# Convolution block with two position networks: first step ahead of its chunk, a place for each chunk of x, and a new order of the loads in the last stretch

## The reference

```
def srms(x): return x / (norm(x) * d ** (-0.5) + EPS)

xn = srms(x)
u = silu(xn @ u_w.T + u_b)              # 96 -> 288 channels
v = silu(xn @ v_w.T + v_b)
a1, a2 = rpe_net(positions, ...)        # two small networks, 256 wide, 3 layers, 128 positions each
out = conv_along_height(v, a2) + conv_along_width(v, a1)   # per channel, by FFT in the reference
out = u * out
return out @ o_w.T + o_b + x
```

## Time and profile before

| | before |
|---|---|
| time, median of 3 runs | 815.77 us (814.77 to 816.03) |
| the profiled execution's own time | 814.11 us |
| its span | 812.3 us |
| PE busy | 749.5 us (92%) |
| ACT busy | 533.9 us (66%) |
| DVE busy | 470.2 us (58%) |
| POOL busy | 282.6 us (35%) |
| moved by DMA | 161.11 MB, mean 198 GB/s |

### The profile page before, as it was taken

One profiled execution on the slowest core, in us unless ns is written; L12 is line 12 of the kernel. 1 busy time (PEld: TensorE's weight loads), 2 busy tenths in 40 slices (PEclk: granted clock), 3 DMA queues, 4 the chain that ended last, 5 costly groups with the idle time before them and its releaser, 6 DMA issues.

```text
span 812.3 us, 19208 instructions
## 1 busy us (share of the span) xinstructions
PE 749.5 (92%) x7148; PEld 672.2 (83%) x7148; DVE 470.2 (58%) x845; ACT 533.9 (66%) x866; POOL 282.6 (35%) x187
## 2 busy tenths in 40 slices
PE   0999997998999999899999999989999998987887
PEld 0999886988999998799999999979999998765655
DVE  6566542336898886444444454445455553776666
ACT  0566574775666666677777877746666666655554
POOL 4333333212212112655555555410000001966764
PEclk9999998999999999999999999989999999999999
DMA  9555554369889786488988888776555555688786
GB/s 209 159 156 156 156 134 138 160 199 215 187 193 200 160 187 191 144 272 272 270 271 262 266 275 271 231 202 144 133 134 131 136 134 185 200 250 248 247 262 193
DMA packets 132017, 161.11 MB, mean 198 GB/s; under 512 B 69484, under 2 KB 97132, under 8 KB 131948
## 3 DMA queue, kind: packets, MB, share of 16 engines
q1 hardware_dynamic: 131948, 160.15, 70.6%
HBM read 109.49 MB, written 50.63 MB: 197 GB/s over the span
## 4 chain that ended last, share of the span: by engine, by line
PE 75%; DMA 13%; DVE 4%; issue 2%; POOL 2%; SPq 2%; ACT 1%; ACTq 0%; DVEq 0%; POOLq 0%
PE ps L974 22%; PE ps L1049 15%; PE ps L1021 9%; PE ps L1034 9%; DMA out<-x_e 9%; PE ps L994 7%; PE ps L984 6%; PE ps L965 3%; DMA stage<-a_dram 2%; PE ps L997 1%; POOL u_in L504 1%; DMA u_dram<-u_in 1%; SPq L300 1%; PE ps L948 1%; DMA free_rows<-in_x 1%
## 5 line engine op out<-in xcount | busy, mean ns | idle before, releaser
L504 POOL TENSOR_TENSOR u_in<-u_in,v 128x1152 f32<-128x1152 f32 (+2 forms) x66 | 174.6, 2651 | 177.5 <-DMA u_in<-u_dram 161.0
L876 DVE TENSOR_TENSOR g<-ps,g 128x512 fp32r<-128x512 f32 (+1 forms) x192 | 125.7, 681 | 74.9 <-ACT g L571 45.8
L832 DVE COPY toepB<-stage 64x512 f32<-64x512 f32 x144 | 105.2, 730 | 80.1 <-PE ps L1049 72.6
L1049 PE MATMUL ps<-toepB,vt 128*128 128x128 f32 x1152 | 141.8, 277 | 0.9 <-POOL toepB L488 0.5
L1049 PEld LDWEIGHTS ps<-toepB,vt 128*128 128x128 f32 x1152 | 136.3, 194 | 1.4 <-POOL toepB L488 0.7
L974 PE MATMUL ps<-wu,xh 97*128 97x288 f32 x512 | 123.6, 307 | 2.1
L766 DVE TENSOR_TENSOR xl<-ps,xh 96x512 fp32r<-96x512 f32 x64 | 43.9, 687 | 140.5 <-ACT xh L544 140.5
L974 PE MATMUL ps<-wv,xh 97*128 97x288 f32 x512 | 120.8, 311 | 2.3 <-ACT u_in L548 1.3
L984 PE MATMUL ps<-ident,u_in 128*128 128x128 f32 (+1 forms) x768 | 102.2, 276 | 21.3 <-POOL u_in L504 20.3
L984 PEld LDWEIGHTS ps<-ident,u_in 128*128 128x128 f32 (+1 forms) x768 | 81.7, 127 | 36.8 <-DVE g L876 12.7
L548 ACT ACTIVATE v<-ps 128x576 f32 (+1 forms) x128 | 83.5, 652 | 38.2 <-PE ps L974 28.7
(11 more groups left out here) (79 smaller groups left out, 1006.5 us busy)
## 6 DMA issues: line engine op xcount, KB each, us to landing
stage<-a_dram SPq DMA_DIRECT2D x144, 256.0 KB, 4.3
u_in<-u_dram SPq DMA_DIRECT2D x64, 576.0 KB, 5.3
u_dram<-u_out SPq DMA_DIRECT2D x48, 576.0 KB, 3.3
x_e<-in_x_eT SPq DMA_DIRECT2D x64, 192.0 KB, 3.8
out<-x_e SPq DMA_DIRECT2D x64, 192.0 KB, 3.8
u_dram<-u_in SPq DMA_DIRECT2D x16, 576.0 KB, 2.8
x_n<-in_x SPq DMA_DIRECT2D x16, 384.0 KB, 5.4
xa<-in_x SPq DMA_DIRECT2D x64, 96.0 KB, 4.6
```

What stands on the lines that cost most here:

```text
L504: return nc.gpsimd.tensor_tensor(out=tile, in0=tile, in1=v[:, start // 2:end // 2, bass.ds(t * NB, NB)].rearrange("p c n e -> p n c e"), o ...
L832: nc.vector.tensor_copy(toepB[n % 2][rows, :, rows], stage[n % STAGES][rows, axis].rearrange("p k c -> p c k")[:, :, ::-1]).then_inc(toepB ...
L876: nc.vector.tensor_tensor(out=low, in0=ps[0:w, bank], in1=high.bitcast(f32), op=ALU.subtract).then_inc(gl_ready, 1)
L1049: last = nc.tensor.matmul(ps[:, SET_BANK[n % 2] + c // NB, (c % NB) * P:(c % NB + 1) * P], vt[n % 2][:, c], toepB[n % 2][:, c], start=Fals ...
```

## The change

Three edits, and a renumbering of counters that follows from them.

1. Start. Chunk 0 is loaded in two parts: step 0 alone (`x_first_loaded`), then steps 1 to 3. DVE squares, sums and norms step 0 by itself (batch 0), and PE projects it as soon as v's weights are split; steps 1 to 3 are a second batch. The position rows (`r_h`) and `rpe_square`, which stood ahead of and right behind the first norms on DVE, come after the second batch. POOL scales step 0 first and then squares steps 1 and 2 of chunk 0; DVE squares step 3. PE's `project(0)` is ahead of `transpose_x(1)` and `rpe_part(0, 0)`, and ACT's `high_x(1)` behind the silus of step 0. All counts of `norms_summed` and `norms_ready` rise by one.
2. A place of its own for each late chunk: chunk 4 in rows of v's space behind the weights (columns that are written from step 20 on), chunks 5, 6, 7 in three places in `x_late`. Chunk 7 is loaded in `phase_a(4)`, without the wait for the scalings.
3. Last stretch. SP's body is now: load u of step t + 3, store the result of step t - 2, wait for the store of step t - 4, load x_e of step t.

```diff
@@ -88,7 +88,8 @@
         OB = OW + 2 * RC * NCH
         RH = OB + 2 * NCH
         RSQ, RIN, W_RAW = RH + 2 * RC, RH + 4 * RC, RH + 6 * RC
-        assert W_RAW + 2 * NCH <= D // 2
+        X_FREE = W_RAW + 2 * NCH
+        assert X_FREE + CHUNK_ROWS <= D // 2
 
         def lw_row(n, o, layer, c):
             return LW + ((n * RC + o) * LAYERS + layer) * RC + c
@@ -112,13 +113,16 @@
 
         g = place("g", [P, 5, TOK], V + 36864, f32r)
         g1 = [place(f"g1{k}", [P, 5, TOK], V + 26624 + 12288 * k, f32r) for k in range(2)]
-        x_late = [place(f"x_late{k}", [P, CHUNK_ROWS, E], V + offset) for k, offset in enumerate((36864, 13824, 0))]
+        x_late = [place(f"x_late{k}", [P, CHUNK_ROWS, E], V + offset) for k, offset in enumerate((0, 13824, 36864))]
 
         def x_chunk(c):
 
             if c < FREE_CHUNKS:
                 return rows(CHUNK_ROWS * c, CHUNK_ROWS, E)
-            return x_late[(c - FREE_CHUNKS) % 3][:]
+            if c == FREE_CHUNKS:
+
+                return free_rows[:, X_FREE:X_FREE + CHUNK_ROWS, 1, P - E:P]
+            return x_late[c - FREE_CHUNKS - 1][:]
 
         x_n = place("x_n", [P, CH * NB, E], V + 22528)
 
...
@@ -246,7 +250,11 @@
                 for i in range(2):
                     sp.dma_start(x_chunk(c)[H * i:H * i + H], rows_of(0, CH * c, CH, i)).then_inc(x_all_loaded, 16)
 
-            load_x_all(0)
+
+            for first, steps, loaded in ((0, 1, x_first_loaded), (1, CH - 1, x_all_loaded)):
+                for i in range(2):
+                    sp.dma_start(x_chunk(0)[H * i:H * i + H, NB * first:NB * (first + steps)],
+                                 rows_of(0, first, steps, i)).then_inc(loaded, 16)
             sp.dma_start(r_pw[:, 0], pos_w).then_inc(pos_loaded, 16)
             sp.dma_start(r_pw[:, 1], pos_b).then_inc(pos_loaded, 16)
             for n, (weight, bias) in enumerate(((v_wT, v_b), (u_wT, u_b))):
...
@@ -319,12 +327,8 @@
                                  ).then_inc(stage_loaded[k], 16)
 
             def phase_a(c, first, last):
-                if c + 3 < CHUNKS - 1:
+                if c + 3 < CHUNKS:
                     load_x_all(c + 3)
-                elif c + 2 == CHUNKS - 1:
-
-                    sp.wait_ge(x_scaled, CH * (c + 2 - 2))
-                    load_x_all(c + 2)
                 for r in range(CH):
                     if last and r == 2:
                         sp.wait_ge(a_stored, 32)
...
@@ -401,12 +405,11 @@
                         if not (first and r == 0) and not (last and r > 0):
                             sp.wait_ge(y_transposed, NCH * STEPS + NCH * t)
                             load_u(1, t + 3, r + 3)
-                        if not (first and r < CH - 1) and not (last and r == CH - 1):
-                            up = (r + 1) // CH
-                            sp.wait_ge(o_stored[1][(r + 1) % CH], 16 * c + 16 * up)
-                            load_xe(1, t + 1, r + 1)
                         if not first or r >= 2:
                             store_out(1, t - 2, r + 2)
+                        if not first:
+                            sp.wait_ge(o_stored[1][r], 16 * c)
+                            load_xe(1, t, r)
                 for c in range(CHUNKS):
                     body(c, c == 0, c == CHUNKS - 1)
                 for t in range(STEPS - 2, STEPS):
@@ -443,12 +446,12 @@
                 nc.gpsimd.tensor_tensor(out=xa[r % 2][:], in0=source, in1=factor, op=ALU.mult).then_inc(x_scaled, 1)
 
             def scale_a0(t, c, r):
-                pool.wait_ge(norms_ready, c + 1)
+                pool.wait_ge(norms_ready, c + 2 if t else 1)
                 wait(pool, x_transposed, t - 1)
                 scale(t, x_chunk(c)[:, NB * r:NB * (r + 1)], r)
 
             def scale_a1(t, loads, chunk, r):
-                pool.wait_ge(norms_ready, CHUNKS + chunk + 1)
+                pool.wait_ge(norms_ready, CHUNKS + chunk + 2)
                 pool.wait_ge(xa_loaded[r % 2], 32 * loads)
                 scale(STEPS + t, xa[r % 2][:], r)
 
@@ -456,25 +459,27 @@
                 nc.gpsimd.tensor_tensor(out=target, in0=source, in1=source, op=ALU.mult).then_inc(squared, 1)
 
             def square_a0(c, r):
-
-                if r == 0:
+                if r == 0 or c == 0:
                     pool.wait_ge(x_all_loaded, 32 * (c + 1))
-                    wait(pool, norms_summed, c)
+                    pool.wait_ge(norms_summed, c + 1)
                 square(x_chunk(c)[:, NB * r:NB * (r + 1)], x_sq[:, NB * r:NB * (r + 1)])
 
             def square_a1(j):
                 pool.wait_ge(xn_loaded, 32 * (j + 1))
                 square(x_n[:], x_n[:])
 
-            for r in range(2):
+
+            scale_a0(0, 0, 0)
+            for r in range(1, CH - 1):
                 square_a0(0, r)
             for r in range(CH - 2):
                 square_a0(1, r)
 
             def phase_a(c, first, last):
                 for r in range(CH):
-                    scale_a0(CH * c + r, c, r)
-                    if first and r == 0:
+                    if not (first and r == 0):
+                        scale_a0(CH * c + r, c, r)
+                    if first and r == 1:
                         square_a0(1, CH - 2)
                         square_a0(1, CH - 1)
                     if c < CHUNKS - 2:
@@ -575,12 +580,15 @@
             def phase_a(c, first, last):
                 for r in range(CH):
                     t = CH * c + r
-                    if not (last and r == CH - 1):
+                    start = first and r == 0
+                    if not start and not (last and r == CH - 1):
                         high_x(t + 1, r + 1)
                     for pair in range(2):
                         silu_v(0, t, pair)
                     for pair in range(2):
                         silu_u(0, t, pair, u_tile(0, r), ua_stored[r % 2], 16 * (2 * c + r // 2) if isinstance(c, int) else 32 * c + 16 * (r // 2))
+                    if start:
+                        high_x(1, 1)
             chunks(act, phase_a)
 
             def phase_c(half):
...
@@ -718,16 +713,16 @@
                 nc.vector.reduce_sum(n_tmp[:, 0, 0:steps * NB], x2, axis=AX.X).then_inc(norms_summed, 1)
 
             def sum_a0(c):
-                sum_squares(CH, x_sq[:], c, CH * (c + 1))
+                sum_squares(CH, x_sq[:], c + 1, CH * (c + 1) - 1)
 
             def sum_a1(j):
-                sum_squares(CH, x_n[:], CHUNKS + j, CH * CHUNKS + j + 1)
+                sum_squares(CH, x_n[:], 1 + CHUNKS + j, CH * CHUNKS + j)
 
             def norms_a0(c, layer=None):
-                return norms(CH * c, CH, c, layer)
+                return norms(CH * c, CH, c + 1, layer)
 
             def norms_a1(j):
-                return norms(STEPS + CH * j, CH, CHUNKS + j)
+                return norms(STEPS + CH * j, CH, 1 + CHUNKS + j)
 
             def run(pieces):
                 for piece in pieces:
@@ -766,9 +761,15 @@
                 nc.vector.tensor_tensor(out=xl[r % 2][0:E], in0=ps[0:E, bank], in1=xh[r % 2][0:E].bitcast(f32),
                                         op=ALU.subtract).then_inc(xl_ready, 1)
 
-            sum_a0(0)
-            run(norms_a0(0))
-            rpe_square()
+            def square_x(r):
+                x_step = x_chunk(0)[:, NB * r:NB * (r + 1)]
+                return nc.vector.tensor_tensor(out=x_sq[:, NB * r:NB * (r + 1)], in0=x_step, in1=x_step, op=ALU.mult)
+
+
+            dve.wait_ge(x_first_loaded, 32)
+            link(square_x(0))
+            nc.vector.reduce_sum(n_tmp[:, 0, 0:NB], x_sq[:, 0:NB], axis=AX.X).then_inc(norms_summed, 1)
+            run(norms(0, 1, 0))
 
             dve.wait_ge(weights_loaded, 4 * 16)
             for n, w in enumerate((wv, wu)):
@@ -777,7 +778,24 @@
                 nc.vector.tensor_copy(high, raw).then_inc(w_split, 1)
                 dve.wait_ge(w_split, 2 * n + 1)
                 nc.vector.tensor_tensor(out=low, in0=raw, in1=high.bitcast(f32), op=ALU.subtract).then_inc(w_split, 1)
-            low_x(0, 0)
+                if n == 0:
+                    dve.wait_ge(x_all_loaded, 32)
+                    square_x(CH - 1).then_inc(squared, 1)
+                    low_x(0, 0)
+
+
+            dve.wait_ge(squared, CH - 1)
+            nc.vector.reduce_sum(n_tmp[:, 0, 0:(CH - 1) * NB], x_sq[:, NB:CH * NB], axis=AX.X).then_inc(norms_summed, 1)
+            run(norms(1, CH - 1, 1))
+
+            dve.wait_ge(pos_loaded, 2 * 16)
+            dve.wait_ge(positions, 2)
+            for n in range(2):
+                for c in range(RC):
+                    last = nc.vector.tensor_scalar(r_h[:, n, c], r_pos[:], r_pw[:, 0, n, c:c + 1],
+                                                   r_pw[:, 1, n, c:c + 1], ALU.mult, ALU.add)
+            link(last)
+            rpe_square()
 
             def phase_a(c, first, last):
                 networks = isinstance(c, int) and c <= LAYERS
@@ -1000,17 +1018,24 @@
             pe.wait_ge(consts_ready, 3)
```

(30 more changed lines are left out.)

## The result

| | before | changed |
|---|---|---|
| median of the runs | 815.27 us | 788.43 us (787.38 to 791.33) |
| ratio | | 0.9681 (0.9648 to 0.9715) |
| the profiled execution, its span | 814.11, 812.3 us | 791.33, 789.5 us |

The change makes the kernel 3.2% faster, 26.0 us by the ratio. The forecast was 797.2 us in a range of 788 to 806, so the time lies at the lower end of the range, outside the likeliest case's own 794 to 801, and nearest to the rival in which PE sets the last stretch (792.3). The profiled execution of the changed kernel is the slowest of its four, that of before one of the faster ones: between the two spans lie only 22.8 us.

The account below looks back on a forecast made before the run. The prediction took the last stretch to be held by a 4.05 us circle of output store and x_e load on SP. Terms: -16.6 + 0.3 - 3.3 + 1.0 = -18.6 us, from 815.77 to 797.2 us, range 788 to 806.

Parts of the forecast that it names:

- the likeliest case: Last stretch: DMA sets a step at 3.02 to 3.3 us; 794 to 801 us in total, chance 0.48.
- the rival in which PE sets the last stretch: Last stretch: PE limits a step at 2.945 us, 21.5 us less there; 792.3 us in total, chance 0.28.
- The circle in the last stretch: SP's load of x_e waits for an output store issued one body before, 4.05 us a step; the new order removes it.
- Its size: Last stretch: 24 steps fall from 3.84 to 3.15 us each, 16.6 us less.
- One sign that I had named for being wrong: DMA: the prediction is wrong if the queue carries more than 334 GB/s.
- my second case: Last stretch: at 425 GB/s DMA would need 2.3 us a step, and PE would set it at 2.945.
- Landings: Last stretch, rival: x_e and u land late, 5.75 us, a step takes 3.5 us; 805.6 us in total, chance 0.19.
- Chunk 7: Its earlier load removes 7.9 us of pause and cold clock, adds 2.6 and 2.0: 3.3 us less.
- The start: Step 0 is projected earlier, but step 1 waits for chunk 2: no gain, 1.0 us more (0 to +2.5).
- The 0.3 for the very end: End of the last stretch: the last x_e is issued some 3 us ahead of use, landing 3.5: 0.3 us more.

Follow-up runs that it names:

- last_only: The kernel before with the third edit alone (SP's order in the last stretch): 792.63 us, ratio 0.9712 to the kernel before.
- short_pe: The changed kernel with one of three matmuls left out for both full blocks of the last stretch's output projection: 785.93 us, ratio 0.9649 to the kernel before.
- x_e_twice: The changed kernel with every load of x_e in the last stretch from step 4 on made twice: 806.56 us, ratio 0.9908 to the kernel before.
- place_only: The kernel before with the second edit alone (a place for each late chunk, chunk 7 loaded one chunk sooner): 812.40 us, ratio 0.996.
- early_seven: The changed kernel with chunk 7 loaded ahead of the store of the networks' result instead of behind it: 792.24 us, ratio 0.9713 to the kernel before.
- late_square: The changed kernel with POOL scaling step 2 before its first square of chunk 2: 790.16 us, ratio 0.9695 to the kernel before.
- split_store: The changed kernel with chunk 7 loaded after step 15's store of u, the networks' store split behind those of steps 16 and 18: 784.02 us, ratio 0.9618.
- split_and_late: The changed kernel with the edits of split_store and late_square together: 782.83 us, ratio 0.9595 to the kernel before.

## Why the prediction came out as it did

**The circle in the last stretch: right.** The place and the 4.05 us are what the traces show; last_only gives 23.5 of the 26 us by it.

**Its size: the term that was off.** I took 3.15 us a step, from "windows with a share near 1 moved 326 and 292 GB/s", as if a share of 1 were the ceiling and the windows of the fused stretch were at it. They were not: there PE set the pace, and DMA moved what was asked. Asked for more, the same queues carry 331 GB/s at a share of 1.02, 336 in last_only, 341 in short_pe, and 329 at 1.07 in x_e_twice. At 0.983 MB a step that is 2.88 to 2.99 us, against PE's 2.945. One sign that I had named for being wrong, a queue that carries more than 334 GB/s, came in last_only and short_pe. The 24 steps took 3.01 us each, not 3.15 and not 2.945: 24 x (3.84 - 3.01) = 19.9 us by the traces where 16.6 were forecast. So the truth lies between my likeliest case and the rival "PE is the limit", much nearer to the latter. In last_only it is that rival, 2.946 us a step up to step 29. The time fell in the range because the range held that rival, not because DMA set the step as I had it.

**The rate of my second case.** The Trainium skill ("DMA: Bandwidth & Descriptors", Bandwidth) gives 425 GB/s, which would have left DMA room; its figure is for one load of 16 MB. The transfers here are of 192 to 576 KB, and in this stretch no run comes to more than 341 GB/s. By 425 GB/s the 1.18 MB of a step in x_e_twice would take 2.8 us, an estimate, and cost nothing; they cost 18.5 us. For this mix the measurement decides.

**Landings: priced right, dismissed too far.** The rival's circle over two steps needs (landing + 1.25) / 2. I set it against a step of 3.15 us, where it binds from a landing of 5.1 us on. Against the real step of 2.945 us, and with the 1.1 us that the chain shows for sum, issue and hand-over, it binds from 4.8 us on, and x_e lands at 4.8 (median). So in the changed kernel this circle and PE are level, and the end of the chain runs through it; one landing of 6.54 us near the end makes a round of 7.65. Its price against PE alone is small here, at most 24 x (3.01 - 2.945) = 1.6 us in this trace, so the rival's 805.6 us did not come about. But in x_e_twice and short_pe the same circle is what the chain shows, so neither run prices DMA's rate by itself.

**Chunk 7: right in mechanism and size.** 7.9 us removed, 2.6 added to the landing, 2.0 for the clock, net 3.3; the measured edit alone is 3.3 (2.0 to 4.4), the store of u landed at about 119.3 against my 118.3, and PE's pause was 4.1 us (4.12 in place_only). What I did not see is that it does not help to put the chunk ahead of the small pieces instead of behind them: early_seven is what I would have advised.

**The start: right that it brings nothing, and nearly why.** Chunk 2 came at 24.5 (I took 24.9), project(1) began at 26.94 (27.7) at half clock. I put 1.0 us on it; alone it measures 0.7 (-0.5 to 1.8). Executions with the same start differ by 1.3 us here, so neither the size nor its sign is established beyond that.

**The sum.** -20 (last stretch, by the traces) + 0.3 - 3.3 + 1.0 gives -22, near the 22.8 us by which the two profiled executions differ. The 0.3 for the very end is not seen: from the transposes of step 31 to the end of the span it is 8.2 us before and 8.3 after. The runs differ by 26.0. For the remaining 3 to 4 us I have no mechanism; 2.9 of them are what the profiled execution of the changed kernel lay above its median. From first to last transposes the last stretch took 92.0 us in last_only, 92.6 in late_square, 93.0 in the changed kernel and 94.3 in split_store, with the same instructions. The chain from 712 to 772 us has no load of x_e in last_only; these loads have 60% of it in late_square, 35% in the changed kernel and 78% in split_store. So the circle takes part in the three slower ones, though not in step with their times; what brings it on in one execution and not in another was not tried.

## What to carry to other kernels

When a queue that issues everything waits for the landing of something it issued itself one iteration ago, the iteration is as long as that landing; look for the store and the load that alternate in the chain, wait for the store of an iteration earlier, and put the wait behind the next issue. A DMA share near 1 in a stretch where an engine sets the pace is no ceiling: price a step by a stretch that asks for more, or keep both prices. When one circle is broken, work out the next one against the step that is hoped for, not against a cautious one: here it was level with PE at once. Before a large transfer is moved to where it fits, look at what stands behind it in the queue and who waits for that, since everything ahead of it delays it.

## What the runs showed of the hardware

- The share of DMA in the windows goes above 1 under load (1.02 to 1.07 at 329 to 341 GB/s, and 1.59 with 91 GB/s moved while small pieces and x mixed, in early_seven), so it is no measure of the room left.
- Landings grow with the load. With 249 GB/s moved (before, 712 to 750 us) u, x_e and the output landed after 5.5, 3.5 and 3.6 us; with 331 (changed) after 6.2, 4.8 and 4.5; in x_e_twice, at 329 with more bytes queued, after 7.5, 6.1 and 5.6.
- Pieces of 32 bytes are slow and hold what is issued behind them: in the kernel before the 288 KB of the networks' result moved at some 55 GB/s for over 5 us, and the store of u behind them took 7.50 us to land, where the one ahead of them in the changed kernel took 3.2.
- A pause of PE of 1.3 us (before, near 116 us) left the granted clock at 1.00; those of 4.1 us (changed) and 5.6 us (before) were followed by 0.50, and so was one of 2.2 us in split_and_late. After a cold start the level was regained at different times in executions of the same code, between 29.5 and 32.6 us by the pace of the matmuls, which moves the end of the start by 1.3 us; what decides it stays open.
